# Gated unit and state-space stage unrolled over the batches, with one addition moved from VectorE to GpSimd

## The reference, cut to what matters

```
# gated unit (per batch)                        xn = layernorm(layernorm(x)) * ln_w + ln_b
uv = silu(xn @ uv_w.T + uv_b);  u, v, base = split(uv, [256, 512])
q, k = rope(base * gamma[c] + beta[c])          # c = 0, 1
kern = square(relu(q @ k.T / sqrt(128) + toeplitz))
x = layernorm(x) + x + (u * (kern @ v)) @ o_w.T + o_b

# state-space block (per batch), 256 channels, 16 states
xs, z = split(layernorm(layernorm(x)) @ W_in.T);  u = silu(conv4(xs))
dt, B, C = split(u @ W_xproj.T);  delta = softplus(dt @ W_dt.T + b_dt)
for n in 16:  h_n = scan(h = exp(delta*A_n)*h + delta*u*B_n);  y += h_n * C_n
x = layernorm(x) + x + ((y + u*D) * silu(z)) @ W_out.T
```

## Time and profile before

| | us |
|---|---|
| median of 3 runs (3761.12 to 3766.71) | 3764.24 |
| the profiled execution's own time | 3772.41 |
| its span, first to last instruction | 3769.2 |
| gated unit, from 1594.9 to 1948.5 | 353.6 |
| state-space stage, from 2225.6 to 3044.1 | 818.5 |
| PE busy / DVE busy / ACT busy / POOL busy, whole span | 2795.5 / 2229.2 / 1601.7 / 707.9 |

### The profile page before, as it was taken

How to read it: one execution, slowest core, us unless ns; L and a number is a source line. 1 busy time by engine, 2 the same in 40 slices (tenths; PEclk the granted TensorE clock), 3 DMA queues, 4 the chain that set the end, 5 groups by cost and what they waited for, 6 DMA issues and landing times.

```text
span 3769.2 us, 55186 instructions
## 1 busy us (share of the span) xinstructions
PE 2795.5 (74%) x18720; PEld 1601.4 (42%) x18720; DVE 2229.2 (59%) x4893; ACT 1601.7 (42%) x2886; POOL 707.9 (19%) x926
## 2 busy tenths in 40 slices
PE   2998899899899926367762636666665688888888
PEld 1666566566566626333332622222222253233225
DVE  2564555455456431355553238889796988777754
ACT  1665566476466502111100314242433333666672
POOL 2000000000000064300016332212121221222221
PEclk9999999999999958688875867778777798999998
DMA  5000000000000011100001210000000034011000
GB/s 157 1 0 2 1 0 1 2 1 0 2 1 0 12 39 52 39 0 0 0 4 39 60 28 0 0 0 0 0 0 0 0 116 157 2 47 47 2 2 23
DMA packets 65897, 78.75 MB, mean 21 GB/s; under 512 B 9005, under 2 KB 41948, under 8 KB 65712
## 3 DMA queue, kind: packets, MB, share of 16 engines
q1 hardware_dynamic: 56816, 60.10, 4.9%
q0 software_dynamic: 8896, 16.29, 1.6%
HBM read 43.58 MB, written 35.52 MB: 21 GB/s over the span
## 4 chain that ended last, share of the span: by engine, by line
PE 28%; DVE 15%; issue 13%; POOL 4%; another core or an unknown queue 3%; ACT 2%; DVEq 0%; DMA 0%; POOLq 0%; SPq 0%; ACTq 0%
DVE Wqkv L1737 4%; PE ps L1613 3%; PE ps L844 3%; PE ps L971 2%; PE ps L590 2%; PE ps L838 2%; PE ps L579 2%; DVE arena L1433 2%; PE ps L1585 1%; DVE arena L1438 1%; POOL arena L1465 1%; PE ps L1574 1%; PE ps L980 1%; POOL slots_in L749 1%
## 5 line engine op out<-in xcount | busy, mean ns | idle before, releaser
L431 DVE CUSTOM_DVE_ANT_0 arena<-ps,causal 128x512 f32<-128x512 f32 (+3 forms) x512 | 282.7, 589 | 345.3 <-PE ps L247 343.8
L355 ACT ACTIVATE arena<-ps 128x512 f32<-128x512 f32 (+1 forms) x640 | 337.8, 548 | 321.7 <-PE ps L260 318.9
L368 ACT ACTIVATE arena<-arena 128x640 f32<-128x640 f32 (+7 forms) x512 | 393.8, 770 | 36.7 <-DVE arena L431 32.7
L1737 DVE TENSOR_REDUCE Wqkv<-ps 128x2 f32<-128x1024 f32 (+3 forms) x384 | 353.3, 953 | 87.1 <-PE ps L1578 81.7
L260 PE MATMUL ps<-ident,arena 128*128 128x128 f32 x2304 | 359.5, 283 | 46.1 <-ACT arena L368 44.6
L1693 ACT ACTIVATE arena<-ps 128x1024 f32<-128x1024 f32 (+3 forms) x384 | 302.3, 809 | 163.0 <-PE ps L1585 159.3
L281 PE MATMUL ps<-arena,rope 128*64 128x128 f32 x4608 | 350.5, 282 | 0.0
L1433 DVE TENSOR_TENSOR_SCAN arena<-arena 128x1024 f32<-128x1024 f32 x128 | 318.9, 2532 | 9.2 <-ACT arena L1379 4.7
L260 PEld LDWEIGHTS ps<-ident,arena 128*128 128x128 f32 x2304 | 249.0, 141 | 177.0 <-issue 144.2
L1308 PE MATMUL ps<-arena,ident 128*128 128x512 f32 x512 | 281.7, 702 | 0.0
L281 PEld LDWEIGHTS ps<-arena,rope 128*64 128x64 f32 x4608 | 242.3, 136 | 74.8 <-issue 64.1
(11 more groups left out here) (259 smaller groups left out, 4824.0 us busy)
## 6 DMA issues: line engine op xcount, KB each, us to landing
arena<-q_dram SPq DMA_DIRECT2D x4, 2048.0 KB, 8.8
arena<-k_dram SPq DMA_DIRECT2D x4, 2048.0 KB, 14.1
q_dram<-arena SPq DMA_DIRECT2D x24, 256.0 KB, 3.7
k_dram<-arena SPq DMA_DIRECT2D x24, 256.0 KB, 3.8
arena<-slots_in SPq DMA_DIRECT2D x8, 640.0 KB, 4.5
slots_out<-arena SPq DMA_DIRECT2D x8, 640.0 KB, 3.9
slots_in<-arena POOLq DMA_DIRECT2D x4, 640.0 KB, 7.9
W<-in_m_W_dram SPq DMA_DIRECT2D x1, 2048.0 KB, 9.9
```

The lines of the kernel that those rows point to most:

```text
L355: nc.scalar.activation(k.probT[:, n % 2, b0 * P:(b0 + nb) * P], k.ps[:, 4 + m % 2, 0:nb * P], ACT.Copy)\
L368: nc.scalar.activation(k.prob[:, i % 2, h, 0:w], k.prob[:, i % 2, h, 0:w], ACT.Exp, bias=k.neg_max[:, i % 2, h:h + 1], scale=-1.0, accum_o ...
L431: ins = nc.vector.tensor_tensor_reduce(k.prob[:, i % 2, h, 512 * g:512 * g + w], k.ps[:, banks[h], 0:w], k.causal[:, first:first + w], 1.0 ...
L1737: nc.vector.tensor_reduce(k.least[:, g, a, i % 4, c, :], k.ps[:, 2 * (m % 3):2 * (m % 3) + 2, 0:search_width(i, c)], AX_X, ALU.min)\
```

## The change

- The barrier after each batch is gone from both stages. Each is now straight code over the 4 batches, with semaphore counts that run through; one barrier stands at the end of each. The inner loop over the 16 states is straight code too.
- `dve_norm_piece` cuts the two normalisations into 12 pieces. DVE runs the pieces of batch b+1 between the blocks u (gated unit) or the states n (state-space stage) of batch b. POOL's two roots per batch follow them; in the state-space stage they stand after L1465's counterpart of states 3 and 9.
- PE transposes the tiles of b+1 before it mixes step 7 of b (gated unit), or after the drive of state 15 of b (state-space stage); then it starts the projections of b+1 before it projects the results of b. DVE convolves half 0 of b+1 before it gates b, and half 1 after.
- The results are projected into two whole PSUM banks and added to X by two additions of 512 columns instead of eight of 128. The projection waits for all four gating instructions.
- In the gated unit DVE makes q and k before it adds v's bias. ACT makes the two affine maps of base before the Silus of u.
- In the state-space stage POOL adds XN to X (128x1024) right after its multiplication of state 1; DVE waits for it (`x_base`) before its piece 4 overwrites XN. ACT scales u by D instead of DVE. dt, B and C come from one group of 112 columns. Ln, the sum and the product for delta*u are made per half.
- z has four buffers; h lies in W1, conv and ud in W2, xs in Wqkv, XN2s in Wo, since those weights are no longer needed.

```diff
+def dve_norm_piece(nc, k, dve, ch, sm, b, piece, out):
+    if piece in (0, 1, 6, 7):
+        for t in range(4 * (piece % 2), 4 * (piece % 2) + 4):
+            last = nc.vector.bn_stats(k.bn6[:, t, :], (k.X_all[:, 8 * b + t, :] if piece < 2 else k.XN[:, t, :]))
+        ch.link(last)
+    elif piece in (2, 8):
+        for t in range(8):
+            last = nc.vector.bn_aggr(k.mv[:, t, :], k.bn6[:, t, :])
+        ch.link(last)
+        nc.vector.tensor_scalar(k.var_eps[:], k.mv[:, :, 1], EPS, None, ALU.add).then_inc(sm[("var1", "var2")[piece // 8]], 1)
+    elif piece in (4, 5, 10, 11):
+        dve.wait_ge(sm[("rstd1", "rstd2")[piece // 10]], b + 1)
...
 # pe_gau
+    for b in range(k.B):
+        for j in range(8):
+            scores(b, j)
+            if j >= 1:
+                mix(b, j - 1)
+        if b + 1 < k.B:
+            pe.wait_ge(sm["biased"], 16 * b + 14)
+            pe_tokens(nc, k, pe, sm, b + 1, k.XN2)
+        mix(b, 7)
+        if b + 1 < k.B:
+            base(b + 1)
+            gate(b + 1)
+            rotated(b + 1)
+        results(b)
+        if b + 1 < k.B:
+            value(b + 1)
...
 # pe_mamba
+        for n in range(NSTATE):
+            if n + 1 < NSTATE:
+                spread_b(b, n + 1)
+            spread_c(b, n)
+            if n >= 1:
+                add_y(b, n - 1)
+        if b + 1 < k.B:
+            pe.wait_ge(sm["dbx0"], 16 * b + 16)
+            pe.wait_ge(sm["b"], 16 * b + 16)
+            pe_tokens(nc, k, pe, sm, b + 1, k.XN2s)
+            project(b + 1, 0)
+        add_y(b, NSTATE - 1)
+        if b + 1 < k.B:
+            project(b + 1, 1)
+            project(b + 1, 2)
+            project(b + 1, 3)
+        results(b)
...
 # dve_mamba
+    for b in range(k.B):
+        split_bc(b)
+        step_size(b)
+        drive(b, 0)
+        for n in range(NSTATE):
+            step(b, n)
+            if n + 1 < NSTATE:
+                drive(b, n + 1)
+            if b + 1 < k.B and n < 12:
+                if n == 4:
+                    dve.wait_ge(sm["x_base"], b + 1)
+                dve_norm_piece(nc, k, dve, ch, sm, b + 1, n, k.XN2s)
+        if b + 1 < k.B:
+            convolve(b + 1, 0)
+        gate(b)
+        if b + 1 < k.B:
+            convolve(b + 1, 1)
+        add_results(b)
...
 # pool_mamba
+            nc.gpsimd.tensor_tensor(k.h[:, 2 * (n % 2) + 1, :], k.du[:, 1, :], k.b_row[:, n % 2, :], ALU.mult)\
+                .then_inc(sm["dbx1"], 1)
+            if n == 1:
+                pool.wait_ge(sm["var2"], b + 1)
+                X = k.X_all[:, 8 * b:8 * b + 8, :]
+                nc.gpsimd.tensor_tensor(X, X, k.XN[:], ALU.add).then_inc(sm["x_base"], 1)
+            if n in (3, 9) and b + 1 < k.B:
+                pool_norm_root(nc, k, pool, sm, b + 1, n // 9)
```

More of the change, by code:

```diff
@@ L857, in act_gau @@
[L857 to L877, removed]
@@ L917, in dve_add_tiles, with half @@
[L917 to L928, removed]
+def half(ap, g):
+    return ap[:, g * 512:(g + 1) * 512]
@@ new lines, in dve_norm_piece @@
+def dve_norm_piece(nc, k, dve, ch, sm, b, piece, out):
[10 more added lines that the diff above has]
+        dve.wait_ge(sm[("rstd1", "rstd2")[piece // 10]], b + 1)
+        if piece == 10 and b >= 1:
+            dve.wait_ge(sm["xnT_ps"], 2 * b)
+        for t in range(4 * (piece % 2), 4 * (piece % 2) + 4):
+            src, dst = (k.X_all[:, 8 * b + t, :], k.XN[:, t, :]) if piece < 10 else (k.XN[:, t, :], out[:, t, :])
+            last = nc.vector.tensor_scalar(dst, src, k.mv[:, t, 0:1], k.rstd[:, t:t + 1], ALU.subtract, ALU.mult)
+        if piece < 10:
+            ch.link(last)
+        else:
+            last.then_inc(sm["xn2"], 1)
+    elif piece == 12:
+        X = k.X_all[:, 8 * b:8 * b + 8, :]
+        ch.link(nc.vector.tensor_tensor(X, X, k.XN[:], ALU.add))
@@ new lines, in act_mamba @@
+        act.wait_ge(sm["soft"], 3 * b + 1)
+        for c in range(2):
+            nc.scalar.activation(k.soft[:, c, :], k.soft[:, c, :], ACT.Ln, bias=1.0).then_inc(sm["soft"], 1)
+        for n in range(NSTATE):
+            N = 16 * b + n
+            act_take_b(nc, k, act, sm, N)
+            for c in range(2):
+                if n == 0:
+                    act.wait_ge(sm["delta"], 2 * b + c + 1)
+                if N >= 2:
+                    act.wait_ge(sm["scan"], N * 2 - 3 + c)
+                nc.scalar.activation(k.da[:, 2 * (n % 2) + c, :], k.delta[:, c, :], ACT.Exp,
+                                     scale=k.A_neg[:, c, n:n + 1]).then_inc(sm["da"], 1)
@@ L1442, in dve_mamba, with gate @@
-    dve.wait_ge(sm["du"], 1)
-    drive(0, 0)
-    mamba_states(dve, step)
-    dve.wait_ge(sm["y_acc"], 2 * NSTATE)
-    for g in range(2):
-        for c in range(2):
-            nc.vector.tensor_tensor(k.h[:, c, g * 512:(g + 1) * 512], k.ps[:, 4 + 2 * c + g, :],
-                                    k.z[:, c, g * 512:(g + 1) * 512], ALU.mult).then_inc(sm["gated"], 1)
-    dve_add_tiles(nc, k, dve, ch, sm, (0, 1), stats=False)
+    def gate(b):
+        dve.wait_ge(sm["y_acc"], 32 * (b + 1))
+        for g in range(2):
+            for c in range(2):
+                nc.vector.tensor_tensor(half(k.h[:, c, :], g), k.ps[:, 4 + 2 * c + g, :], half(k.z[:, 2 * (b % 2) + c, :], g),
+                                        ALU.mult).then_inc(sm["gated"], 1)
@@ new lines, in drive, with step @@
+    def drive(b, n):
+        N = 16 * b + n
+        dve.wait_ge(sm["b"], N + 1)
+        if n == 0:
+            dve.wait_ge(sm["du"], 2 * b + 1)
+            if b >= 1:
+                dve.wait_ge(sm["y_ps"], 2 * b)
+        if N >= 2:
+            dve.wait_ge(sm["y_acc"], N * 2 - 3)
+        nc.vector.tensor_tensor(k.h[:, 2 * (n % 2), :], k.du[:, 0, :], both(k.ps[:, 0:2, :]), ALU.mult)\
+            .then_inc(sm["dbx0"], 1)
+    def step(b, n):
+        N = 16 * b + n
+        for c in range(2):
+            dve.wait_ge(sm["da"], N * 2 + c + 1)
+            dve.wait_ge(sm[("dbx0", "dbx1")[c]], N + 1)
+            h = k.h[:, 2 * (n % 2) + c, :]
+            nc.vector.tensor_tensor_scan(h, k.da[:, 2 * (n % 2) + c, :], h, 0.0, ALU.mult, ALU.add).then_inc(sm["scan"], 1)
+        dve.wait_ge(sm["c_ps"], N + 1)
+        for c in range(2):
+            dve.wait_ge(sm["scan"], N * 2 + c + 1)
+            h = k.h[:, 2 * (n % 2) + c, :]
+            nc.vector.tensor_tensor(h, h, both(k.ps[:, 2:4, :]), ALU.mult).then_inc(sm["prod"], 1)
@@ new lines, in dve_mamba @@
+    for piece in range(12):
+        dve_norm_piece(nc, k, dve, ch, sm, 0, piece, k.XN2s)
+    dve.wait_ge(sm["pad"], 1)
+    convolve(0, 0)
+    convolve(0, 1)
+    for b in range(k.B):
+        split_bc(b)
+        step_size(b)
+        drive(b, 0)
+        for n in range(NSTATE):
+            step(b, n)
[3 more added lines that the diff above has]
+                if n == 4:
+                    dve.wait_ge(sm["x_base"], b + 1)
+                dve_norm_piece(nc, k, dve, ch, sm, b + 1, n, k.XN2s)
+        if b + 1 < k.B:
+            convolve(b + 1, 0)
+        gate(b)
+        if b + 1 < k.B:
+            convolve(b + 1, 1)
+        add_results(b)
```

646 lines of the change are left out of this document (338 added, 308 removed).

## The result

The changed kernel takes 3557.64 us (median of 4 runs, 3554.57 to 3562.06), the one before 3764.07 beside it: ratio 0.9453, interval 0.9436 to 0.9469, so 206 us less. One execution, the fourth of experiment 10, took 4771.66 us at a granted clock of 0.55 and is left out of that experiment's ratio.

The account below looks back on a forecast made before the run. Serial transitions bound both stages, with DVE the bound engine in the state-space stage. Gated unit 92.5 plus state-space stage 73.9 makes 166.4 us less: 3772.4 becomes 3606.0, and the median, 8.2 lower, 3598 us; range 3570 to 3645.

Parts of the forecast that it names:

- Gated unit: Gated unit: a batch takes 60.0 us against 88.6, normalisation pieces hidden in gaps; 92.5 us less in all.
- Stalls become 4 for states 0 to 11, 2 for states 12 to 14, 2 for the two roots: State-space steps: scan stalls behind POOL's late multiplication, 8.7 us a batch before, become 8 including the roots.
- The pieces: State-space steps: normalisation pieces on DVE, statistics, normalising and aggregation, cost 9.9 us a batch with their waits.
- Transition: State-space stage, end of drive 15 to end of next drive 0: 43.8 us against 76.7, 32.9 less.
- The first batch: State-space stage: first batch 5.7 us less, from one group of 112 columns and shorter delta.
- the last batch: State-space stage: 1.2 us more for the last addition to X.
- the end: State-space stage: 1.6 us more at the last end.
- The addition on POOL: State-space stage: POOL's addition to X makes a scan wait 0.6 us, 1.2 in the last batch; bounds 0 and 2.35.
- The roots: State-space steps: POOL's two roots, 1.64 us each, cost 2 us a batch; bounds 0 and 3.3.
- POOL's share: Rival: every root and addition on POOL lies fully on the scans and normalising pieces stall too; 3620 us, chance 0.17.
- a low clock: Rival: longer states leave PE idle, each begins at the low clock and POOL is always late; 3640 us, chance 0.10.
- The best case: State-space stage: no stalls of scans at all, 8 us a batch better than forecast; 3566 us, chance 0.03.

Follow-up runs that it names:

- experiment 10: Kernel before with batch and state loops as straight code, barriers kept, plus three buffers for POOL's half of h: ratio 0.9917 to the kernel before.
- experiment 3: Changed kernel plus useless DVE statistics of four tiles after each of states 0 to 11 in the last state-space batch: ratio 0.9453 to the kernel before.
- experiment 4: Changed kernel with all 12 state-space normalisation pieces in one bunch after state 11: ratio 0.9530 to the kernel before.
- experiment 5: Changed kernel with three buffers instead of two for POOL's half of h, so POOL waits for older TensorE additions: 3554.2 us.
- experiment 6: Changed kernel with the addition of XN to X back on DVE, after the drive of state 4, instead of on POOL: 3569.9 us.

## Why the prediction was wrong, point by point

The profiled execution was forecast at 3606.0 and took 3554.6, 51.4 less. Of these, 10.5 are the untouched stages, 5 the gated unit, and 34.4 the state-space stage; the last 1.4 lie outside the profiled span (3772.4 - 3769.2 before, 3554.6 - 3552.8 after).

- **Gated unit: right.** Forecast 92.5 less, measured 97.6, alone 97.5. The pieces were hidden, q and k no longer bound, v's bias and Silu come last in the transition. Of the 2 us a batch that it was shorter than forecast, 1.3 come from the transposes at the full clock, for which I took the duration after an idle PE.
- **"Stalls become 4 for states 0 to 11, 2 for states 12 to 14, 2 for the two roots": this step failed.** The cause was read rightly, the size was not. Of the forecast 8 us a batch 3.2 came (130.0 - 119.3 - 7.6), which is 14 of the missing 51 us and the largest single part. They are 1.1 in state 0, 0.5 in state 1 behind the addition to X, 0.6 to 0.9 in state 4, up to 0.4 in state 5, where a normalising piece ran beside POOL, and 0.5 in state 14.
  - I moved the next scans back by one piece, that of the same state. But POOL's late multiplication hangs on PE, and PE starts at the drive before it. Between the end of that drive and the scans that POOL could disturb lie two pieces. The earlier one delays the scans, products and drive, the later one the next scans. In state 4 of the last batch of experiment 3 POOL ended 9.40 us after that drive and the scans began at 9.48; with one piece of 0.7 they would have begun at 8.8, before POOL's end.
  - PE was also quicker than the rows before gave. In state 6 of batch 0 the two short groups ahead of PE's additions took 0.6 us each instead of 1.0, and POOL ended 8.75 us after the drive, not 9.41 as in the earlier trace rows. In state 14, with no piece near it, the stall fell from 1.3 to 0.5.
  - Experiment 3 shows that a piece takes the stalls away and experiment 4 that they come back without it; 5 and 10 show that POOL's wait for PE is the cause. How much the second piece and how much the quicker PE is worth was not taken apart.
  - The stall in state 0 is new. Before, the first scans waited 1.17 us for ACT's exponentials, and POOL ended as they began. Now POOL's multiplication (2168.69 to 2171.04) waits for the second half of delta*u and reaches into the scans that begin at 2169.78. Every version with the new stage has a first pair of 5.6 us; nothing here tried to remove it.
- **The pieces: mis-sized.** 9.9 forecast. From scans to scans in states without a stall a piece of statistics adds 0.7 us (8.66 - 7.95), the aggregation 0.6, a normalising piece 0.8 to 1.0: 7.6 a batch. A piece also fills the 0.1 us that the scan waits after the drive. In one bunch the same work costs 13.0, 3.5 of it waits for the roots.
- **Transition: mis-sized.** 32.9 less forecast from drive to drive, 36.1 measured (40.6 instead of 76.7); by the scans it is 37.2. PE made the additions of states 14 and 15 at the full clock and gave the projection 3.1 us earlier than I had it (convolution 8.0 us after the last drive, not 11.1). The other 1.1 by the scans are the wait for ACT named above, which is gone. The forecast had counted that wait among the stalls: of its 8.7 us before, 7.7 were stalls of scans.
- State span and transition together are 3 x (3.0 - 37.2) = -102.6 against the forecast -71.0. The first batch gained 10.0 (first scans after 50.6 us instead of 60.6), not 5.7; in the profiles with 54.1 it would be 6.5, so this part can't be judged from one profile; the last batch lost 2.3 and the end 1.9 (1.2 and 1.6 forecast).
- **The addition on POOL: right.** The forecast price was 0.6 us a batch and 1.2 in the last; the scans of state 1 took 0.5 and 1.2 longer, and leaving it out gave 1 us in all. The alternative, the addition on DVE at its own 1.2 us a batch, is the costlier one here: 7 to 8 us in experiment 6, but 1.3 with three buffers. The rule of the Trainium skill ("SBUF — State Buffer", Who interferes with whom), by which a DVE instruction with two SBUF inputs waits for the whole of a GpSimd instruction that was issued first, agrees in both directions here: DVE's addition took 2.87 us behind POOL in experiment 6, and POOL's root, 1.64 us alone, lasted 3.56 beside a scan that had begun 0.17 us before it.
- **The roots: too dear, within the bounds.** Forecast 2 us a batch, bounds 0 and 3.3; no scan was seen to wait for one. The root of 3.56 us waited itself, and the pair of scans beside it took 4.47. The multiplication behind it came late (2203.54, scans 5.06 in state 4), but POOL had stood idle 2.60 us for PE's L1405, and with three buffers that pair took 4.47 with the root in the same place.
- **The rivals.** POOL's share and a low clock would each have made it slower; both effects exist, but the change relieved them instead of adding to them. The best case, "no stalls of scans at all", had 3566 and a chance of 0.03; it was nearest by number only: 3.2 us of stalls a batch remain, and 10 in the last, while the transitions, pieces and first batch were shorter than it had them. The range was too narrow on the fast side: it had no bound for stalls that go without the rest staying as forecast, nor for a PE at the full clock in the transitions.

## What to carry to other kernels

Count the cover of a stall from the event that releases the late engine, with everything that now lies between, not only what lies in the same iteration. Useful work between two dependent instructions of the bound engine can cost nothing where that engine stalled anyway: spread it, since the same pieces in one bunch cost 31 us of the stage more. Where a change fills TensorE's idle time, take the durations of its full clock as one end of the range.

## What the runs showed of the hardware that was not expected

- TensorE's two clocks put the state loop into a cycle of two. After 4.7 us of idle time the eight additions took 5.1 to 5.2 us and released POOL late; POOL held up the scans by 1.2; the next gap of TensorE was then 1.1 us, its additions took 3.6, and POOL was in time. An added 0.7 us a state ended the stalls, not the cycle: in the last batch of experiment 3 TensorE still went between additions of 4.7 to 5.3 us behind 4.2 us of idle time and additions of 3.6 behind 2.5 (states 6 to 12), and it went on alternating with three buffers too.
- Taking away a stall elsewhere returned less than its length: 16 of 28.6 us in experiment 10, 4.0 of 12.4 in experiment 5. In experiment 5, behind the states of the last batch without stalls, the last eight additions took 6.75 us, as eight such records did at a granted clock of 0.55 (6.63). What sets the clock exactly at that point was not tried.
- The same code before the first scans took 50.6 to 51.0 us in six profiles with the new stage and 54.1 in three. The executions of one kernel scatter over 3 to 14 us, perhaps for this reason; that it is the phase of TensorE's clock is argued from durations (PE's group for delta took 7.2 us in experiment 6 and 3.7 in the full change), not shown by an experiment of its own.
